# Edge masks as PE's stationary operand, sums turned back on PE, tree sums on DVE, and scatters after the degree loop, in a graph convolution kernel

## The chip, the cores and the metric

The kernel runs on one core of one Trainium2 chip. The metric is the device time of one execution in microseconds (us). The core has five engines with queues of their own: PE (TensorE, matmuls and weight loads), DVE (VectorE), ACT (ScalarE), POOL (GpSimd) and SP (SyncE, which here only issues DMAs). They wait for each other through semaphores: an instruction waits until a counter has a value, and a finished instruction adds to one. A difference of 0.5% (15.5 us) is about what a measurement of this kernel can tell from none.

## The reference

```python
def gcn_conv(x, src, dst, w, W, b, n):
    xw = x @ W
    deg = jax.ops.segment_sum(w, dst, num_segments=n)
    dinv = jnp.where(deg > 0, jax.lax.rsqrt(deg), 0.0)
    norm = dinv[src] * w * dinv[dst]
    return jax.ops.segment_sum(xw[src] * norm[:, None], dst, num_segments=n) + b
# gnn: edges + one loop edge of weight 1 for each node
out = relu(gcn_conv(x, src, dst, w, W1, b1, n))
out = gcn_conv(out, src, dst, w, W2, b2, n)
out = relu(batch_norm(out) * gamma + beta + identity)
# all: x is (6250, 256) float32; 100000 edges, dst sorted
x = x + gnn(layernorm(x), edges)
# ffn: softmax over 8 experts, the two best, gelu, hidden size 512
x = x + ffn(layernorm(x))
```

## The kernel before

The 6250 nodes are 49 tiles of 128 rows. The 100000 edges, sorted by target, are tiles of 128, and 14 edge tiles (`GT`) are a group; there are 56 groups, and each one's targets lie within 128 nodes. The product with `W` comes after the sum over edges, so a layer is: scale the nodes' rows (`y`), store them as a table in DRAM, sum over edges into `acc` in SBUF (features on partitions, nodes along the columns), and multiply.

The 56 groups are summed in two ways. 16 of them (`DG`) are *dense*: a matrix of pair weights (`pairs` in DRAM, first filled with zeros by SP, then POOL *scatters* each edge's weight into its cell, L479, 224 scatters of 128 cells) is loaded by SP in *units* (L374, `load_pairs`, 256 KB each, seven slots ahead), and PE multiplies the node rows by it (L1272, two matmuls of 128x512 a unit, 196 units a layer). As several edges may fall into one cell, DVE first sums the weights of edges with equal source and target (the *pair sums*, L781 to L791): for 40 distances, eight at a time in five chunks, it compares keys (L781), multiplies by the weights (L783) and reduces, by maximum to learn whether an edge's cell has been had before (L784) and by sum for the weights (L787).

The other 40 groups (`GG`) are *sparse*: POOL *gathers* the source rows (L492, 14 gathers of 128 rows a group, into one of two halves of `G`), DVE builds for each edge tile a 128x128 *mask* of weights by target (L908), and PE multiplies (L1287): the gathered rows are the weights that PE holds, two blocks of 128 columns, and the mask moves. The sum comes out with features on partitions, and DVE adds it into `acc` (L932). POOL's gathers of group k wait until the sum of group k-2 is done (`summed`), PE's start of group k until that sum is added (`added`). The first 28 gathers of a layer wait for no sum.

Order on PE within a layer: the *self-turn* (L1260, 98 transposes that turn `y` tiles for the loop edges; DVE copies each out, L901, and PE waits for the copy of the tile two back), then `BEFORE` dense units, then the groups, with `PER_GROUP` units spread between a group's edge tiles. Before all this come the pair sums, the splits of edge weights into bf16 parts (L829, L832), and the *degree loop*: 56 half-turns in which DVE prepares a group (L842, L843, L845) and PE multiplies (L1224, 14 small matmuls), two buffers, each half waiting for the other engine. Then the scales (L851 to L890), `y` (L895 on DVE, L611 on ACT), the table's store on SP (L381), and POOL's gathers after that store. POOL's scatters wait only for the cell numbers (`cells_set`, L807) and the zeros (`filled`). The order is written out by hand in each engine's program.

## Time and profile before

| what | value |
|---|---|
| median of 3 runs | 3099.36 us (3092.58 to 3104.66) |
| the profiled execution | 3096.93 us, its span 3095.1 us |
| PE, matmuls | 2158.0 us busy, 70% of the span |
| PE, weight loads | 1539.0 us, 50% (beside the matmuls) |
| POOL | 1676.4 us, 54% |
| DVE | 901.8 us, 29% |
| ACT | 377.0 us, 12% |
| mean granted clock of PE | 0.889 of full speed |

The span in the page's order of time: edges loaded, pair sums and splits to 122.8 us; degree loop to 470; `y` stored to 490; self-turn and first dense units to 673.7, when the first group's sum is added; the groups of layer 0 to 1450, of layer 1 to 2354 (its own self-turn and gathers start at 1508); batch norm, layer norm, router and the expert layers to the end. "Busy" counts an engine's execution of instructions, not its waits. In rows of time, the bracket names how long the engine was idle before the instruction and what released it; "remote" is a release whose source the profile doesn't know, "issue" means that it waited for nothing that the profile shows.

### The profile page before, as it was taken

To read this page: it belongs to the slowest core of one execution; us is meant where nothing else is said; L and a number is where in the kernel's file an instruction comes from. 1 tells how busy PE (TensorE), PEld (TensorE's weight loads), DVE (VectorE), ACT (ScalarE), POOL (GpSimd) and SP (SyncE) were. 2 spreads that over 40 slices of the span, in tenths; PEclk is the share of its full clock that TensorE was granted. 3 is DMA by queue.
4 is the path that set the end of the run, shared out by engine and by line. 5 is a ranking of instruction groups with operands and counts; after the bars stand their busy time and mean duration, and the time that the engine had idled before them with its cause. 6 is when DMAs were issued, how large, how long until landed. Compare 5 with 4: busy or idle time off the path is not lost.

```text
span 3095.1 us, 34624 instructions
## 1 busy us (share of the span) xinstructions
PE 2158.0 (70%) x10692; PEld 1539.0 (50%) x10693; DVE 901.8 (29%) x2587; ACT 377.0 (12%) x1053; POOL 1676.4 (54%) x1782
## 2 busy tenths in 40 slices
PE   0100046998888788646598788888888666899897
PEld 0100033455555555535365455555555562788887
DVE  8700055011222211212332212222123676233332
ACT  6000001000000000001200000000000562333333
POOL 1677703016666666663346666666665430566665
PEclk9999999998888888767889899999999755999999
DMA  9940005544544444332445555555555023677775
GB/s 325 329 144 1 0 0 163 158 136 143 145 145 141 143 142 144 95 92 80 131 123 158 147 154 157 156 155 155 153 160 168 24 77 103 169 189 175 180 176 135
DMA packets 264392, 431.24 MB, mean 139 GB/s; under 512 B 39664, under 2 KB 147887, under 8 KB 264143
## 3 DMA queue, kind: packets, MB, share of 16 engines
q1 hardware_dynamic: 181455, 253.80, 26.1%
q0 software_dynamic: 81088, 173.80, 21.9%
q10 hardware_dynamic: 1728, 2.13, 0.2%
q8 instruction: 64, 1.05, 0.1%
q14 instruction: 57, 0.47, 0.0%
HBM read 339.36 MB, written 91.16 MB: 139 GB/s over the span
## 4 chain that ended last, share of the span: by engine, by line
another core or an unknown queue 28%; PE 23%; POOL 17%; DVE 13%; issue 11%; DMA 6%; POOLq 1%; DVEq 1%; SPq 1%; ACT 1%; ACTq 0%
POOL arena L492 14%; PE psum L1272 8%; PE psum L1287 4%; DMA ACC<-rows_for_experts,ACC 4%; DVE arena L908 3%; PE psum L1308 3%; PE psum L1394 2%; PE psum L1402 2%; POOL out_dram L558 2%; PE psum L1369 2%; DMA out_dram<-ACC 1%; PE psum L1224 1%; DVE ACC L845 1%; PE psum L1322 1%
## 5 line engine op out<-in xcount | busy, mean ns | idle before, releaser
L492 POOL DMA_INDIRECT arena<-conv_rows,edge_cols x1120 | 1059.4, 946 | 887.7 <-issue 318.7
L1287 PEld LDWEIGHTS psum<-arena 128*128 128x128 f32 x4480 | 640.9, 209 | 501.6 <-issue 484.8
L1287 PE MATMUL psum<-arena 128*128 128x128 f32 x4480 | 683.4, 296 | 289.9 <-issue 277.3
L1272 PE MATMUL psum<-arena,X 128*128 128x512 f32 x1568 | 815.5, 653 | 43.6 <-DVE ACC L923 26.4
L1272 PEld LDWEIGHTS psum<-arena,X 128*128 128x128 f32 x1568 | 303.3, 211 | 307.3 <-issue 273.3
L932 DVE TENSOR_TENSOR ACC<-ACC,psum 128x256 f32 x80 | 33.8, 422 | 1226.0 <-remote 1085.4
L479 POOL DMA_INDIRECT pair_weights<-scale_b,mean_b x224 | 229.5, 1025 | 156.3 <-DVE mean_b L807 88.3
L908 DVE TENSOR_SCALAR arena<-iota,edge_cols 128x128 f32<-128x128 f32 x1120 | 294.4, 370 | 0.3
L1224 PE MATMUL psum<-ACC 128*128 128x6 bf16 x784 | 56.1, 202 | 318.1 <-DVE ACC L845 299.0
L1394 PE MATMUL psum<-ACC,arena 128*128 128x128 f32 x1680 | 215.8, 284 | 0.2 <-DVE ACC L1154 0.2
L1224 PEld LDWEIGHTS psum<-ACC 128*128 128x128 bf16 x784 | 51.5, 159 | 322.8 <-DVE ACC L845 303.2
L558 POOL DMA_INDIRECT out_dram<-ACC x105 | 167.7, 1597 | 74.2 <-issue 49.2
L1394 PEld LDWEIGHTS psum<-ACC,arena 128*128 128x128 f32 x1680 | 206.8, 201 | 0.6 <-issue 0.6
L1402 PE MATMUL psum<-arena,ACC 128*128 x840 | 199.9, 381 | 0.2 <-ACT ACC L689 0.2
L1402 PEld LDWEIGHTS psum<-arena,ACC 128*128 128x128 f32 x840 | 152.7, 192 | 17.2 <-issue 0.6
L546 POOL DMA_INDIRECT ACC<-rows_for_experts,ACC x105 | 104.9, 999 | 84.8 <-DVE ACC L1141 51.0
L623 ACT ACTIVATE X<-tmp,dinv 128x256 f32<-128x256 f32 x49 | 24.9, 508 | 991.1 <-DVE tmp L971 991.1
L689 ACT ACTIVATE ACC<-psum,b1e 128x128 f32<-128x128 f32 x420 | 119.8, 369 | 164.5 <-PE psum L1394 130.8
L632 ACT ACTIVATE edge_cols<-ACC 128x256 f32 x49 | 18.8, 413 | 915.4 <-DVE ACC L992 914.8
L1172 DVE TENSOR_TENSOR ACC<-psum,b2e 128x256 f32<-128x256 f32 x105 | 44.7, 426 | 267.9 <-PE psum L1402 211.8
L842 DVE COPY ACC<-psum 128x6 f32 x56 | 9.1, 162 | 275.0 <-remote 263.2
L1260 PE MATMUL psum<-ident,X 128*128 128x128 f32 x196 | 50.3, 384 | 52.0 <-DVE ACC L901 27.3
(259 smaller groups left out, 1410.3 us busy)
## 6 DMA issues: line engine op xcount, KB each, us to landing
arena<-pair_weights SPq DMA_DIRECT2D x392, 256.0 KB
arena<-in_L_ffn_W_dram SPq DMA_DIRECT2D x113, 512.0 KB, 7.8
pair_weights<-zeros SPq DMA_DIRECT2D x4, 12544.0 KB, 60.5
arena<-conv_rows,edge_cols POOLq DMA_INDIRECT x1120
conv_rows<-X SPq DMA_DIRECT2D x14, 896.0 KB, 4.8
X<-in_x_dram SPq DMA_DIRECT2D x12, 896.0 KB, 10.4
rows_for_experts<-ACC SPq DMA_DIRECT2D x7, 910.0 KB, 4.3
out_dram<-X SPq DMA_DIRECT2D x6, 896.0 KB
```

The costliest lines, as they stand in the source:

```text
L479: pool.indirect_dma_start(pairs, bass.IndirectOffsetOnAxis(cell_i[:, t:t + 1], 0), cell_w[:, t:t + 1], None).then_inc(paired[b], 16)
L492: pool.indirect_dma_start(G[:, n * D:(n + 1) * D], None, y_tab[layer], bass.IndirectOffsetOnAxis(srcT[:, t:t + 1], 0)).then_inc(gathered[n ...
L546: pool.indirect_dma_start(xs[:, u * DX:(u + 1) * DX], None, rows_x, bass.IndirectOffsetOnAxis(slot_i[:, n:n + 1], 0)).then_inc(xs_in[u], 16)
L558: pool.indirect_dma_start(out, bass.IndirectOffsetOnAxis(slot_i[:, n:n + 1], 0), ys[:, u * D:(u + 1) * D], None, bounds_check=N - 1, oob_i ...
L689: ins = a.activation(hT[:, slot * H + c * P:slot * H + (c + 1) * P], psum[:, 2 + slot, c * P:(c + 1) * P], ACT.Gelu, bias=b1e[:, bass.ds(e ...
L908: v.tensor_scalar(S[:, n * P:(n + 1) * P], iota[:, 0:P], dst_rel[:, t:t + 1], wT[:, t:t + 1], ALU.is_equal, ALU.mult).then_inc(s_ready, 1)
L1224: ins = m.matmul(bank(2 + h, 6), hot[:, :, j], w_group[:, (h * GT + j) * 6:(h * GT + j + 1) * 6], start=(j == 0), stop=(j == GT - 1))
L1272: ins = m.matmul(bank(6 + c, BW), X[:, t * D + c * P:t * D + (c + 1) * P], A_in[:, u * BW:(u + 1) * BW], start=(t == 0), stop=(t == NT - 1))
L1287: ins = m.matmul(bank(2 * (k % 2) + c, P), G[:, n * D + c * P:n * D + (c + 1) * P], S[:, n * P:(n + 1) * P], start=(j == 0), stop=(j == GT ...
L1308: ins = m.matmul(bank(6 + j % 2, D), acc[:, k, bass.ds(q * P, P)], W[:, k * D:(k + 1) * D], start=(k == 0), stop=(k == KC - 1))
L1394: ins = m.matmul(psum[:, 2 + s, c * P:(c + 1) * P], w1s[:, s4 * KC * H + k * H + c * P:s4 * KC * H + k * H + (c + 1) * P], xsT[:, s * D + ...
L1402: ins = m.matmul(bank(4 + s, D), hT[:, s * H + c * P:s * H + (c + 1) * P], w2e[:, bass.ds(e * (HC * D) + c * D, D)], start=(c == 0), stop= ...
```

## The change

Four things, none of which alters what is computed.

1. *Tree sums.* In each of the five chunks the two reductions (L784, L787) become trees of element-wise instructions that halve the eight rows three times: maxima in bf16, sums in f32, and each chunk is joined to a running result, so that L789 to L791 fall away and one copy (L815 after) follows.
2. *The scatters wait for the degrees.* POOL's first scatter also waits for `deg_summed`, which DVE sets behind the degree loop.
3. *Masks as weights.* In a sparse group the mask is PE's stationary operand and the gathered rows move: one 128x256 matmul for each edge tile (L1320 after) instead of two of 128x128. The sum then has nodes on partitions. ACT copies it out of PSUM (L628, new), PE turns it with two transposes (L1306, new, behind the fifth edge tile of the next group), and DVE adds the turned sum (L955). DVE's masks of group k+1 wait for the sum of group k-1.
4. *Dense units.* `BEFORE` goes from 74 to 98 units in layer 0, `PER_GROUP` from 4 to 3.

```diff
-        BEFORE = (74, 0)
-        PER_GROUP = (4, 5)
+        BEFORE = (98, 0)
+        PER_GROUP = (3, 5)
...
                     pool.wait_ge(cells_set, 1)
+                    pool.wait_ge(deg_summed, 1)
...
+                def copy_sums(layer):
+                    for k in range(GG):
+                        act.wait_ge(summed, GG * layer + k + 1)
+                        if GG * layer + k >= 2:
+                            act.wait_ge(sum_turned, GG * layer + k - 1)
+                        a.activation(tmp[:, k % 2 * D:(k % 2 + 1) * D], bank(k % 2, D), ACT.Copy).then_inc(sum_copied, 1)
...
                 for c in range(MAXIN // 8):
...
-                    chain(v.tensor_reduce(had[0:DR, c * RW:(c + 1) * RW],
-                                          sliding(eq8[0:DR, :], HALO - d0, 8, SPAN - 1, RW).rearrange("p d i -> p i d"),
-                                          AX_X, ALU.max))
-                    chain(v.tensor_reduce(parts[0:DR, c * RW:(c + 1) * RW], wsame.rearrange("p d i -> p i d"),
-                                          AX_X, ALU.add))
...
+                    chain(v.tensor_tensor(had3[:, 0:4], sliding(eq8[0:DR, :], HALO - d0, 4, SPAN - 1, RW),
+                                          sliding(eq8[0:DR, :], HALO - d0 + 4 * (SPAN - 1), 4, SPAN - 1, RW), ALU.max))
+                    v.tensor_tensor(had3[:, 4:6], had3[:, 0:2], had3[:, 2:4], ALU.max)
+                    chain(v.tensor_tensor(wsame[:, 0:4], wsame[:, 0:4], wsame[:, 4:8], ALU.add))
...
+                v.tensor_copy(had_f[0:DR, :], had[0:DR, :]).then_inc(pairs_summed, 1)
...
                         def add_group(k):
-                            dve.wait_ge(summed, GG * layer + k + 1)
+                            dve.wait_ge(sum_turned, GG * layer + k + 1)
...
-                            v.tensor_tensor(a, a, psum[:, 2 * (k % 2):2 * (k % 2) + 2, 0:P], ALU.add).then_inc(added, 1)
+                            v.tensor_tensor(a, a, bank(2 + k % 2, D).rearrange("p (c n) -> p c n", c=KC), ALU.add).then_inc(added, 1)
...
                             if k + 1 < GG:
+                                if k:
+                                    dve.wait_ge(summed, GG * layer + k)
                                 build(k + 1)
...
+                        def turn_sum(k):
+                            pe.wait_ge(sum_copied, GG * layer + k + 1)
+                            if GG * layer + k >= 2:
+                                pe.wait_ge(added, GG * layer + k - 1)
+                            for c in range(KC):
+                                ins = m.transpose(bank(2 + k % 2, D)[:, c * P:(c + 1) * P],
+                                                  tmp[:, k % 2 * D + c * P:k % 2 * D + (c + 1) * P], ident[:, :])
+                            ins.then_inc(sum_turned, 1)
...
                             if GG * layer + k >= 2:
-                                pe.wait_ge(added, GG * layer + k - 1)
+                                pe.wait_ge(sum_copied, GG * layer + k - 1)
...
-                                for c in range(KC):
-                                    ins = m.matmul(bank(2 * (k % 2) + c, P), G[:, n * D + c * P:n * D + (c + 1) * P],
-                                                   S[:, n * P:(n + 1) * P], start=(j == 0), stop=(j == GT - 1))
+                                ins = m.matmul(bank(k % 2, D), S[:, n * P:(n + 1) * P], G[:, n * D:(n + 1) * D],
+                                               start=(j == 0), stop=(j == GT - 1))
                                 if j == GT - 1:
                                     ins.then_inc(summed, 1)
+                                if k and j == 4:
+                                    turn_sum(k - 1)
...
+                        turn_sum(GG - 1)
```

PE, layer 0, from the self-turn (L1260, after it L1285) to the first groups; L1272 (L1297) is a dense unit's matmul, L1287 (L1320) an edge tile's, and so many of a kind as stand behind x. Before:

```order
L1260 MATMUL psum<-ident,X 128x128 x98
L1263 COMPARE_AND_BRANCH
L1272 MATMUL psum<-arena,X 128x512 x148
L1287 MATMUL psum<-arena 128x128 x8
L1272 MATMUL psum<-arena,X 128x512 x2
L1287 MATMUL psum<-arena 128x128 x6
L1272 MATMUL psum<-arena,X 128x512 x2
L1287 MATMUL psum<-arena 128x128 x8
```

And after, to the second group's turn of the first group's sum:

```order
L1285 MATMUL psum<-ident,X 128x128 x98
L1288 COMPARE_AND_BRANCH
L1297 MATMUL psum<-arena,X 128x512 x196
L1320 MATMUL psum<-arena 128x256 x5
L1297 MATMUL psum<-arena,X 128x512 x2
L1320 MATMUL psum<-arena 128x256 x5
L1297 MATMUL psum<-arena,X 128x512 x2
L1320 MATMUL psum<-arena 128x256 x4
L1297 MATMUL psum<-arena,X 128x512 x2
L1320 MATMUL psum<-arena 128x256 x5
L1306 MATMUL psum<-ident,tmp 128x128 x2
```

48 dense matmuls have moved ahead of the first group, each group has half as many matmuls for its edge tiles, and the turn stands inside the next group, with the rest of that group queued behind it.

POOL, from the first scatter (`pair_weights`) to the gathers of the third group (`arena<-conv_rows`), with what each waits for. Before:

```order
L479 DMA pair_weights<-scale_b,mean_b 12873728x1 [waits filled0,cells_set]
L479 DMA pair_weights<-scale_b,mean_b 12873728x1 x55
```

After:

```order
L484 DMA pair_weights<-scale_b,mean_b 12873728x1 [waits filled0,deg_summed,cells_set]
L484 DMA pair_weights<-scale_b,mean_b 12873728x1 x55
L484 DMA pair_weights<-scale_b,mean_b 12873728x1 [waits filled1]
L484 DMA pair_weights<-scale_b,mean_b 12873728x1 x55
L484 DMA pair_weights<-scale_b,mean_b 12873728x1 [waits filled2]
L484 DMA pair_weights<-scale_b,mean_b 12873728x1 x55
L484 DMA pair_weights<-scale_b,mean_b 12873728x1 [waits filled3]
L484 DMA pair_weights<-scale_b,mean_b 12873728x1 x55
```

Only the first wait has changed; behind it stand all 224 scatters and then, in the same queue, every gather.

DVE, two successive groups: the masks (`arena<-iota,edge_cols`) of the next group, then the addition of this one's sum. Before:

```order
L908 TENSOR_SCALAR arena<-iota,edge_cols 128x128 x14
L912 TENSOR_LOAD base_i
L912 ISA x2
L932 ISA [waits dense_added,added,summed]
L932 TENSOR_TENSOR ACC<-ACC,psum 128x2x128
```

After:

```order
L931 TENSOR_SCALAR arena<-iota,edge_cols 128x128 [waits summed]
L931 TENSOR_SCALAR arena<-iota,edge_cols 128x128 x13
L935 TENSOR_LOAD base_i
L935 ISA x2
L955 ISA [waits dense_added,added,sum_turned]
```

The addition waits for PE's turn instead of PE's sum, and the masks have a wait of their own.

## Rows read from the trace of the kernel before

**Rows 1.** The page's chain of work that ended last: its first line.
```profile
another core or an unknown queue 28%; PE 23%; POOL 17%; DVE 13%; issue 11%; DMA 6%; POOLq 1%; DVEq 1%; SPq 1%; ACT 1%; ACTq 0%
```

**Rows 2.** Order of time, DVE, degree loop. Columns: start, duration (us), ..., [idle before, releaser].
```profile
299.07 0.16 DVE L842 COPY ACC<-psum 128x6 f32 x1 [37.81 <-remote]
...
338.28 0.17 DVE L842 COPY ACC<-psum 128x6 f32 x1 [37.86 <-remote]
...
429.95 0.16 DVE L842 COPY ACC<-psum 128x6 f32 x1
...
431.24 0.16 DVE L842 COPY ACC<-psum 128x6 f32 x1
...
431.50 1.09 DVE L845 TENSOR_TENSOR ACC<-ACC 128x1792 bf16<-128x1792 bf16 x1
```

**Rows 3.** Order of time, POOL: first and last of 224 scatters, first gather.
```profile
97.26 1.28 POOL L479 DMA_INDIRECT pair_weights<-scale_b,mean_b  x1 [88.27 <-DVE mean_b L807]
...
393.85 0.96 POOL L479 DMA_INDIRECT pair_weights<-scale_b,mean_b  x1 [0.30 <-issue]
...
499.43 0.99 POOL L492 DMA_INDIRECT arena<-conv_rows,edge_cols  x1 [104.63 <-DMA conv_rows<-X]
```

**Rows 4.** Order of time, DVE: two of the self-turn's 49 copies.
```profile
509.97 0.42 DVE L901 COPY ACC<-psum 128x256 f32<-128x256 f32 x1 [0.41 <-PE psum L1260]
...
523.88 0.42 DVE L901 COPY ACC<-psum 128x256 f32<-128x256 f32 x1 [2.37 <-remote]
```

**Rows 5.** Order of time, PE: 42 dense units (168 matmul records).
```profile
540.46 74.92 PE L1272 MATMUL psum<-arena,X 128*128 128x512 f32 x168 [4.65 <-DMA arena<-pair_weights]
```

**Rows 6.** Order of time, POOL: first gather after each of four waits for a sum.
```profile
673.74 0.94 POOL L492 DMA_INDIRECT arena<-conv_rows,edge_cols  x1 [139.00 <-PE psum L1287]
...
693.93 0.94 POOL L492 DMA_INDIRECT arena<-conv_rows,edge_cols  x1 [3.00 <-remote]
...
1299.76 0.94 POOL L492 DMA_INDIRECT arena<-conv_rows,edge_cols  x1 [2.73 <-remote]
...
1341.97 0.94 POOL L492 DMA_INDIRECT arena<-conv_rows,edge_cols  x1 [7.48 <-PE psum L1287]
```

**Rows 7.** Order of time, PE: the last matmuls of one group.
```profile
806.13 1.50 PE L1287 MATMUL psum<-arena 128*128 128x128 f32 x12
```

**Rows 8.** Order of time, DVE: two additions of a group's sum.
```profile
815.17 0.42 DVE L932 TENSOR_TENSOR ACC<-ACC,psum 128x256 f32 x1 [16.27 <-remote]
...
1311.94 0.42 DVE L932 TENSOR_TENSOR ACC<-ACC,psum 128x256 f32 x1 [8.31 <-remote]
```

**Rows 9.** Busy time (and count) of each engine in two stretches, core 0.
```profile
795.03:807.63 12.60, 12.60 (x66) 9.50 (x66) 3.87 (x15) 0.00 (x0) 9.50 (x11) 0.87 0.61 178
1299.76:1306.00 6.24, 5.97 (x38) 5.78 (x36) 3.88 (x15) 0.00 (x0) 4.72 (x5) 0.71 0.29 84
```

**Rows 10.** Order of time, DVE: pair sums, splits, first degree copy.
```profile
64.93 2.69 DVE L781 TENSOR_TENSOR ACC<-arena 112x2432 f32<-112x2432 f32 x1
...
67.66 2.29 DVE L783 TENSOR_TENSOR arena<-ACC,arena 112x2048 f32<-112x2048 f32 x1
...
69.87 3.61 DVE L784 TENSOR_REDUCE ACC<-ACC 112x256 f32<-112x2048 f32 x1
...
89.36 2.31 DVE L789 TENSOR_REDUCE ACC<-ACC 112x256 f32<-112x1280 f32 x1
...
93.93 0.43 DVE L791 TENSOR_TENSOR arena<-arena 112x256 f32<-112x256 f32 x1
...
104.78 7.97 DVE L829 TENSOR_TENSOR ACC<-ACC 128x784 bf16<-128x784 bf16 x3
...
122.76 0.17 DVE L842 COPY ACC<-psum 128x6 f32 x1 [2.01 <-issue]
```

**Rows 11.** The page's groups: busy us, mean ns | idle before, releaser.
```profile
L1287 PE MATMUL psum<-arena 128*128 128x128 f32 x4480 | 683.4, 296 | 289.9 <-issue 277.3
...
L623 ACT ACTIVATE X<-tmp,dinv 128x256 f32<-128x256 f32 x49 | 24.9, 508 | 991.1 <-DVE tmp L971 991.1
```

More of the change, by code:

```diff
@@ L109, in gnn_ffn @@
         eqw = arena[:, at:at + 8 * RW]
-        parts = arena[:, at + 8 * RW:at + (8 + MAXIN // 8) * RW]
-        assert (8 + MAXIN // 8) * RW <= 2 * GT * P
+        wsum = arena[:, at + 8 * RW:at + 9 * RW]
+        cell, hop = [arena[:, at + (9 + n) * RW:at + (9 + n) * RW + DT] for n in range(2)]
+        assert 11 * RW <= 2 * GT * P
         at += 2 * GT * P
@@ L143, in gnn_ffn @@
         tile_f = early(2 * NG)
-        eq8 = early(8 * (HALO + RW))
-        had = early(MAXIN // 8 * RW)
+        eq8 = early(8 * (HALO + RW), BF16)
+        had8 = early(8 * RW, BF16)
+        had, had_f = early(RW, BF16), early(RW)
+        int_f = early(2 * RH)
         assert at <= KC * NP
@@ L612, in _ @@
                                      bias=nb[:, t:t + 1], scale=sc[:, t:t + 1]).then_inc(y0_act, 1)
+                act.wait_ge(flag_set, 1)
+                general = act.value_load(flag_i[0:1, 0:1], min_val=0, max_val=1)
+                def copy_sums(layer):
[4 more added lines that the diff above has]
+                        a.activation(tmp[:, k % 2 * D:(k % 2 + 1) * D], bank(k % 2, D), ACT.Copy).then_inc(sum_copied, 1)
+                with act.If(general == 0):
+                    copy_sums(0)
+                act.wait_ge(agg_done, 1)
                 act.sem_inc(y_ready, 1)
@@ L624, in _ @@
                                      scale=dinv[:, t:t + 1]).then_inc(y_ready, 1)
+                with act.If(general == 0):
+                    copy_sums(1)
                 with act.Fori(0, NCH) as c:
@@ L750, in _ @@
                 dve.wait_ge(ld_rows, 16 * ROW_LOADS)
-                seen, first = eq8[0:DR, 0:RH], eq8[0:DR, RH:2 * RH]
+                seen, first = int_f[0:DR, 0:RH], int_f[0:DR, RH:2 * RH]
                 v.tensor_copy(seen, src_h[0:DR, :])
@@ L1207, in _ @@
                 pe.wait_ge(pairs_summed, 1)
-                for x, rows in enumerate((eq8[0:DR, 0:RW], eqw[0:DR, RW:2 * RW])):
+                for x, rows in enumerate((had_f[0:DR, :], wsum[0:DR, :])):
                     for h in range(2):
```

12 lines of the change are left out of this document (8 added, 4 removed).

## The prediction, as put on record before the kernel was run

> **What bounds the kernel now.** I read the page's chain of waits first: 28% of the span ends on "another core or an unknown queue" on one core, 23% on PE, 17% on POOL, 13% on DVE [rows 1]. A release that the profile can't name, for over a quarter of the span, is the thing to explain. Then I read DVE, PE and POOL in order of time, stage by stage.
>
> *Degree loop.* Each of 56 half-turns is three DVE instructions (L842, L843, L845) and 14 small PE matmuls. Undisturbed, copies L842 follow each other by 1.29 us (429.95, 431.24); while POOL issues the scatters of L479, by 39.2 us (299.07, 338.28), 37.8 of them idle, "remote" [rows 2]. PE's work hasn't grown: what arrives late is its semaphore update. 39.2 us for 14 matmuls and 14 weight loads is 1.40 us per PE instruction. The scatters go out from 97.26 to 393.85, 224 of them, so one per 1.33 us (0.96 busy and 0.30 between in the clean part) [rows 3]. The loop only runs off when they end.
>
> *Self-turn.* It begins fresh on PE, and when POOL gathers from 499.43 on, a tile (two transposes, four PE records) goes, after some 12 us and 15 tiles, from 0.83 us (0.42 busy, 0.41 idle at 509.97) to 2.79 us (0.42 and 2.37 at 523.88) [rows 3, 4]: 0.70 us per PE record. So the lateness again, at half the rate.
>
> *Dense units, then the first sum.* 42 units take 74.92 us, 1.78 each [rows 5]. POOL's third gather group waits 139 us for the first sum, to 673.74 [rows 6].
>
> *Groups.* POOL restarts every 20.2 us (673.74, 693.93): 14 gathers of 1.25 = 17.2 to the end of the last, then 3.00 "remote" [rows 6]. The sum that it waits for is long done: in a like group its last matmul ends at 806.13+1.50 = 807.63, but DVE adds at 815.17 [rows 7, 8]. From POOL's restart at 795.03 to that last matmul PE ran 66 matmul and 66 weight-load records [rows 9]. Where the dense units are over, a sum comes earlier in POOL's stream, within its first 74 records [rows 9], and DVE adds at 1311.94 [rows 8]: late too, but before the 14 gathers are out; POOL then runs two groups on end, 1299.76 to 1341.97, with a pause of 7.48 [rows 6]. So the picture is: in a stream of POOL's issues the first some 70 PE records are answered within 12 to 16 us, later ones 0.7 to 1.4 us apiece, and what is left when POOL stops. The period is set by POOL's issues plus that flush, and PE's own work matters through its number of records, not its length.
>
> The Trainium skill (SBUF — State Buffer, "Who interferes with whom") says that PE and ACT never wait on anyone. Here DVE waits 37.8 us for a PE that has 14 short matmuls to do. If the rule held also for these updates, the first rival below is what comes.
>
> **The change part by part.** All sums are made against the profiled execution, 3096.93 us, 0.1% under the median of 3099.36.
>
> *Tree sums (DVE, on the path to the scatters and the degree loop).* A chunk is L781 2.69, L783 2.29, L784 and L787 some 3.6 each: 12.2 us, five times, then L789 and its twin L790 at 2.3 and L791 0.43 [rows 10]. After: L802 and L804 stay; four f32 adds of 1024, 512, 256 and 256 columns, at L783's 1.12 ns a column and some 0.13 each to start (256 columns took 0.43), are 2.8 us; four bf16 maxima of the same sizes are 1.7 us at L845's rate (1792 columns in 1.09) or 2.8 at f32's [rows 2, 10]. A chunk is 9.5 to 10.6; times five saves 8 to 14; at the end 5.0 become 0.4, 4.6 more. 13 to 19; I take 16, between the two. The Trainium skill (VectorE: DVE Perf Modes, "Mode 2×_1P — pack two bf16 into one 32-bit read") asks for 4-byte alignment, and the first maximum's operands begin at odd columns: by it the maxima would be nearer the dear end, which L845's aligned row can't show.
> The splits after it (L829, L832, six of 2.66 [rows 10]) lay beside scatters; L845's rate gives 0.5 for 784 columns. 0 to 13 less; I take 5. The degree loop starts at 122.76−21 = 102 [rows 10].
>
> *Scatters wait for the degrees.* Degree loop 102 + 56×1.29 + 1.4 ≈ 176. Scatters then, 224×1.263 = 283 us: to 459. The 28 gathers that wait for no sum are behind them in POOL's queue, and y is stored by then: to 494, flushed 3 us later. Queued behind POOL's wait is every gather; the pair loads on SP wait for the scatters block by block (56 each, the first at 247).
> PE meanwhile: before, the self-turn began 14.5 us after the loop's end, so at 190, now under the scatters. Some 15 tiles pass promptly (10 us), 34 tiles of four records go at 1.40 or 0.70: 190 or 95 us, to 390 or 295. A dense unit has eight records, 11.2 or 5.6 us: by 494 9 or 35 units, and some 7 more are in flight. 82 or 56 of the 98 are left, ×1.78 = 146 or 100, and 9 for the rest of the first group: first sum at 652 or 606, against 673.6. The row for a stream of scatters is the 1.40 one; I take 640, **−33**. What covers the 283 us of scatters before is the degree loop, which is held; after, only self-turn and dense, held likewise: a shift of work under the same cover.
>
> *Masks as weights, sums copied and turned.* Per group before: 4480/80 = 56 matmul records and as many weight loads [rows 11], 112, and 32 for dense; now 56 in all, 24 dense, 4 to turn. ACT's copy is about 0.51 (L623, 128x256 f32 [rows 11]), the turn and DVE's add under a microsecond each. Nothing is queued behind ACT's wait but later copies. PE's turn, though, stands after the fifth tile of the next group, and everything of that group is behind it; DVE's masks wait for the sum before. Since PE, blocked at a turn until POOL stops, starts fresh, the next sum is about 60 records into POOL's stream, where it is answered before the 14 gathers are out: POOL runs two groups (28×1.25 = 34.7) and pauses 3.0 (as at 693.93) to 7.5 (as at 1341.97): 18.85 to 21.1 a group. In the latter PE had slow passes to make up, so I take a pause of 4.1, 19.4: 0.8×32 groups = **−26**, three more for the last groups. In layer 1 there are five dense units, 64 records to the sum, and the mask build is held by the turn; two-group and one-group streams mix (38.5+20.2)/3 = 19.6; between 18.85 and 20.5; I take 19.95 for 40 groups, **−10**. At each layer's end copy, turn and add come behind the last sum, 1.5 each: **+3**.
> The longer matmul (256 columns for two of 128) moves as many columns, and POOL's issues, not PE, make the period: nothing. If it cost PE half as much again, that is below 3 us a group (28 matmul records of 0.1 us more each, a third of their mean 0.296 [rows 11]), inside POOL's 17.
>
> Sum: 3096.9−33−26−3−10+3 = **3028 us**.
>
> **Rivals.**
> *A, PE isn't held under scatters that it doesn't read* (held only where a handshake has to come back, say). For: nothing but the half-rate under gathers. Against: 39.2. Self-turn and dense end by about 404, the first sum at 495 when its gathers have landed: −178, with the periods' −36 and +3, 2885.
> *B, slower: the price is per handshake, not per record.* Each half-turn of the degree loop is one PE update that DVE needs, 39 us. The self-turn has one per tile. Then from 190 to 494 only eight tiles pass beyond the prompt 15; after 497 there are 26×0.83 = 22, 98×1.78 = 174 and 9: first sum at 702, +28, no gain in the periods (each group has two more such updates), +3: 3128. For it: nobody but the degree loop measured the scatters. Against: the self-turn's 2.8 us under gathers, one per tile too. It decides when more than about 167 us of PE's work is left at 497.
> *C, the groups stay at 20.2* (PE's turn makes POOL's next sum late as before; each stream 14 gathers): 3096.9−33+3 = 3067. For it: in every stretch with dense units POOL paused after each group.
> *D, the added links lengthen the groups* to the 21.1 of the two-group stream with its 7.48 pause: 3067 + 0.8×72 = 3124.
> *E, POOL never pauses*, 17.5 a group: −2.7×72 = −194, with −33 and +3, 2873.
>
> **How the numbers follow.** Forecast 50%, C 30%, B 8%, A 5%, D 4%, E 3%. Its own range: −67 to −22 for the first sum, −43 to −10 and −54 to +0 for the periods, 2936 to 3068. The range given, 2945 to 3100, takes in C and its upper end; left out are A and E below, B and D above. 0.5% of 3099 (15.5 us) is what a measurement can tell from no change: faster is the forecast, C less its worst, A and E, 80%; same 8%, slower 12%, B and D.
>
> **What would show it.** DVE's degree copies all 1.29 apart; POOL's first scatter at about 176, its first gather right behind the last scatter (459). DVE's self-turn copies 2.8 or 5.6 us apart from about 200 on. First wait for a sum ending at 606 to 652. POOL's gathers in streams of 28 with pauses of 3 to 5 in layer 0. Wrong: copies 39 us apart in the self-turn (B), one pause per 14 gathers (C), a dense part that is over by 404 (A).

## The result, and the profile after

The changed kernel takes 3116.87 us (median of 8 runs, 3112.64 to 3129.26), the one before 3101.02 us (8 runs): ratio 1.0054, 95% interval 1.0034 to 1.0075. It is slower by half a per cent; the forecast was 3028, with a range of 2945 to 3100. The profiled executions' spans are 3115.6 and 3095.1 us, 20.5 apart.

| point in the span (us) | before | after | difference |
|---|---|---|---|
| first scatter | 97.26 | 177.65 | +80.4 |
| degree loop over | 470 | 176 | −294 |
| first gather | 499.43 | 464.93 | −34.5 |
| POOL restarts on the first sum | 673.74 | 690.63 | +16.9 |
| last sum of layer 0 added | 1449.76 | 1453.86 | +4.1 |
| first gather of layer 1 | 1507.76 | 1514.73 | +7.0 |
| last sum of layer 1 added | 2356.67 | 2377.26 | +20.6 |
| end | 3095.1 | 3115.6 | +20.5 |

So 34.5 us gained at the first gather are lost again before the first sum, and 16.9 more; layer 0 gives 12.8 back, layer 1 costs 13.6, the linear stage between them 2.9. The page's chain of waits after (compare [rows 1]):

```profile
PE 31%; another core or an unknown queue 19%; POOL 18%; issue 14%; DVE 9%; DMA 6%; ACT 1%; POOLq 1%; DVEq 1%; SPq 1%; ACTq 0%
```

PE has taken over first place from the nameless releaser, 31% against 23% before, and the nameless share is down from 28% to 19%. The granted clock is no part of the difference: the eight executions have a mean of 0.79 (3112.6 to 3117.4 us) or 0.85 (3114.7 to 3129.3), and 17 executions of the kernel before on one chip, at 0.81 (3088.6 to 3100.7) or 0.89 (3083.2 to 3103.3), don't differ by it either. POOL in order of time (start, duration, engine, line, [idle before, releaser]), the answers to [rows 3, 6]:

```profile
177.65 1.17 POOL L484 DMA_INDIRECT pair_weights<-scale_b,mean_b  x1 [168.64 <-DVE ACC L876]
...
463.67 0.96 POOL L484 DMA_INDIRECT pair_weights<-scale_b,mean_b  x1 [0.30 <-issue]
...
464.93 1.00 POOL L497 DMA_INDIRECT arena<-conv_rows,edge_cols  x1 [0.30 <-issue]
...
690.63 0.95 POOL L497 DMA_INDIRECT arena<-conv_rows,edge_cols  x1 [187.22 <-PE psum L1320]
...
730.59 0.95 POOL L497 DMA_INDIRECT arena<-conv_rows,edge_cols  x1 [5.05 <-remote]
...
750.65 0.95 POOL L497 DMA_INDIRECT arena<-conv_rows,edge_cols  x1 [2.80 <-remote]
...
1973.28 0.95 POOL L497 DMA_INDIRECT arena<-conv_rows,edge_cols  x1 [17.16 <-PE psum L1320]
```

The scatters start at 177.65 (176 was forecast), the gathers follow at once, and the restart is at 690.63, not 640. A stream of 28 gathers is followed by a pause of 5.05, one of 14 by 2.80. POOL is slowed as well at the end of this long stream: its last 25 DMAs are 1.40 us apart and 1.10 busy, where it had been 1.27 and 0.96.

```profile
502.33 1.09 POOL L497 DMA_INDIRECT arena<-conv_rows,edge_cols  x1 [0.30 <-issue]
```

DVE, from the pair sums through the splits and the degree loop to the self-turn [rows 2, 4, 10]:

```profile
64.34 2.69 DVE L802 TENSOR_TENSOR ACC<-arena 112x2432 bf16<-112x2432 f32 x1
...
67.07 2.29 DVE L804 TENSOR_TENSOR arena<-ACC,arena 112x2048 f32<-112x2048 bf16 x1
...
69.28 0.69 DVE L805 TENSOR_TENSOR ACC<-ACC 112x1024 bf16<-112x1024 bf16 x1
...
71.60 0.29 DVE L809 TENSOR_TENSOR ACC<-ACC 112x256 bf16<-112x256 bf16 x1
...
84.27 7.96 DVE L852 TENSOR_TENSOR ACC<-ACC 128x784 bf16<-128x784 bf16 x3
...
102.24 0.17 DVE L865 COPY ACC<-psum 128x6 f32 x1 [2.00 <-issue]
...
103.54 0.16 DVE L865 COPY ACC<-psum 128x6 f32 x1
...
194.52 0.42 DVE L924 COPY ACC<-psum 128x256 f32<-128x256 f32 x1 [0.41 <-issue]
...
225.53 0.42 DVE L924 COPY ACC<-psum 128x256 f32<-128x256 f32 x1 [5.16 <-remote]
...
404.73 0.42 DVE L924 COPY ACC<-psum 128x256 f32<-128x256 f32 x1 [5.17 <-remote]
...
410.34 0.42 DVE L924 COPY ACC<-psum 128x256 f32<-128x256 f32 x1 [5.18 <-issue]
...
421.53 0.42 DVE L924 COPY ACC<-psum 128x256 f32<-128x256 f32 x1 [5.17 <-remote]
```

The degree loop (L865) runs at 1.30 us a half-turn. The self-turn's copies (L924) come every 5.6 us, 404.73 to 410.34: four PE records of 1.40. PE's dense units in the same stretch [rows 5]:

```profile
491.47 3.78 PE L1297 MATMUL psum<-arena,X 128*128 128x512 f32 x4 [7.42 <-DMA arena<-pair_weights]
...
502.51 3.42 PE L1297 MATMUL psum<-arena,X 128*128 128x512 f32 x4 [7.25 <-DMA arena<-pair_weights]
...
531.16 59.38 PE L1297 MATMUL psum<-arena,X 128*128 128x512 f32 x132 [3.86 <-DMA arena<-pair_weights]
...
593.62 86.08 PE L1297 MATMUL psum<-arena,X 128*128 128x512 f32 x196 [3.08 <-DVE ACC L946]
```

A dense unit (x4) comes every 11.0 us (491.47 to 502.51): eight records of some 1.40, though the idle time is put down to the unit's load. That goes on until 531, 27 us after the end of POOL's last gather of this stream (502.33 + 1.09 = 503.4). Then 33 units and, after the block's addition, 49 more are left, 82.

Last, POOL's steady stretch by windows (busy time and count of PE, PE's weight loads, DVE, ACT and POOL, then the granted clock, the DMA share and GB/s): 37 groups (518 gathers) in each layer, in layer 1 after the change 36 (505). After:

```profile
690.63:1429.84 739.21, 502.14 (x1504) 310.68 (x1502) 152.36 (x563) 14.21 (x38) 492.47 (x518) 0.79 0.42 124
1577.29:2321.32 744.03, 599.83 (x1818) 352.21 (x1816) 150.51 (x552) 13.84 (x37) 479.45 (x505) 0.87 0.51 153
```

Before:

```profile
673.74:1424.89 751.15, 563.15 (x2579) 395.61 (x2578) 153.78 (x568) 0.00 (x0) 490.28 (x518) 0.82 0.45 130
1570.52:2324.70 754.18, 629.22 (x2829) 411.24 (x2828) 153.67 (x568) 0.00 (x0) 489.68 (x518) 0.92 0.53 155
```

That is 19.98 us a group instead of 20.30 in layer 0, and 20.6 instead of 20.4 in layer 1, with the granted clock down from 0.82 and 0.92 to 0.79 and 0.87. PE's matmul records fell from 2579 to 1504, and the period moved by 0.3 us.

### The profile page after: what moved, and what is told of

It is laid out like the page before. It is cut to its first block, busy times and chain, and to the rows that moved or that the text cites. A ratio compares the mean times of both kernels' runs of the same rounds, so it can differ in the third digit from the quotient of the medians.

```text
span 3115.6 us, 30733 instructions
## 1 busy us (share of the span) xinstructions
PE 2147.3 (69%) x8612; PEld 1417.5 (45%) x8613; DVE 881.2 (28%) x2615; ACT 408.5 (13%) x1133; POOL 1674.2 (54%) x1782
## 4 chain that ended last, share of the span: by engine, by line
PE 31%; another core or an unknown queue 19%; POOL 18%; issue 14%; DVE 9%; DMA 6%; ACT 1%; POOLq 1%; DVEq 1%; SPq 1%; ACTq 0%
POOL arena L497 16%; PE psum L1297 13%; PE psum L1320 6%; DMA ACC<-rows_for_experts,ACC 4%; PE psum L1344 3%; PE psum L1430 2%; PE psum L1438 2%; PE psum L1405 2%; POOL out_dram L563 1%; DVE arena L931 1%; DMA out_dram<-ACC 1%; DVE ACC L868 1%; PE psum L1249 1%; PE psum L1358 1%
## 5 line engine op out<-in xcount | busy, mean ns | idle before, releaser
L1297 PE MATMUL psum<-arena,X 128*128 128x512 f32 x1568 | 819.2, 650 | 195.7 <-issue 95.3
L1320 PE MATMUL psum<-arena 128*128 128x256 f32 x2240 | 631.2, 413 | 203.0 <-issue 174.8
L1320 PEld LDWEIGHTS psum<-arena 128*128 128x128 f32 x2240 | 457.4, 208 | 445.7 <-issue 368.1
L1297 PEld LDWEIGHTS psum<-arena,X 128*128 128x128 f32 x1568 | 319.6, 207 | 517.3 <-issue 383.6
L955 DVE TENSOR_TENSOR ACC<-ACC,psum 128x256 f32 x80 | 33.8, 422 | 1247.9 <-remote 802.9
L484 POOL DMA_INDIRECT pair_weights<-scale_b,mean_b x224 | 217.9, 973 | 237.7 <-DVE ACC L876 168.6
L628 ACT ACTIVATE tmp<-psum 128x256 f32<-128x256 f32 x80 | 30.7, 384 | 2093.4 <-remote 1089.6
L1285 PE MATMUL psum<-ident,X 128*128 128x128 f32 x196 | 53.2, 380 | 231.7 <-issue 136.8
L1285 PEld LDWEIGHTS psum<-ident,X 128*128 128x128 f32 x196 | 25.6, 182 | 258.8 <-issue 252.1
L924 DVE COPY ACC<-psum 128x256 f32<-128x256 f32 x98 | 40.2, 423 | 243.0 <-remote 196.1
L1306 PE MATMUL psum<-ident,tmp 128*128 128x128 f32 x160 | 36.0, 311 | 77.6 <-ACT tmp L628 70.1
L946 DVE TENSOR_TENSOR ACC<-ACC,psum 128x256 f32 x32 | 13.5, 420 | 265.4 <-PE psum L1297 256.3
```

The costliest lines, as they stand in the source:

```text
L484: pool.indirect_dma_start(pairs, bass.IndirectOffsetOnAxis(cell_i[:, t:t + 1], 0), cell_w[:, t:t + 1], None).then_inc(paired[b], 16)
L1285: ins = m.transpose(bank(4 + t % 2, D)[:, k * P:(k + 1) * P], X[:, t * D + k * P:t * D + (k + 1) * P], ident[:, :])
L1297: ins = m.matmul(bank(6 + c, BW), X[:, t * D + c * P:t * D + (c + 1) * P], A_in[:, u * BW:(u + 1) * BW], start=(t == 0), stop=(t == NT - 1))
L1320: ins = m.matmul(bank(k % 2, D), S[:, n * P:(n + 1) * P], G[:, n * D:(n + 1) * D], start=(j == 0), stop=(j == GT - 1))
```

## The experiments

The theory drawn from this trace (theory 1) is that what POOL issues is finished more slowly than POOL issues it, one DMA per 1.40 (scatters) to 1.43 us (gathers) against 1.26 and 1.25, and that while the surplus is open, PE's updates come one by one behind it. It would explain at once why the hold outlasts a stream by a time that grows with the stream's length: 2.80 after 14 gathers, 5.05 after 28, 27 after 252 DMAs. It also gives 14 × 1.43 = 20.0 for a group with either form of matmul. The rivals: PE is held for as long as POOL issues at all (theory 3, the prediction's); the wait alone cost the 17 us (theory 2). Runs of one letter share a chip, on which the kernel before ran as well, so ratios are compared, not times.

### Taking the wait away, or putting only it in; issuing more slowly

The run e1 takes the wait out of the changed kernel, and e4 puts it alone into the kernel before:

```diff
                     pool.wait_ge(cells_set, 1)
-                    pool.wait_ge(deg_summed, 1)
```

e2 and e3 put a small instruction behind every DMA of POOL; `paced` counts only POOL's own memsets:

```diff
+                def breathe(times):
+                    for _ in range(times):
+                        pool.wait_ge(paced, count[0])
+                        g.memset(pace[:, :], 0.0).then_inc(paced, 1)
+                        count[0] += 1
...
                         pool.indirect_dma_start(pairs, bass.IndirectOffsetOnAxis(cell_i[:, t:t + 1], 0),
                                                 cell_w[:, t:t + 1], None).then_inc(paired[b], 16)
+                        breathe(1)
```

> The changed kernel without the scatters' wait for the degree loop; all else as changed. Theory 1 (POOL's DMAs are finished one per 1.40 to 1.45 us whatever else runs, 252 of them from 177.65 to 531 in the changed kernel; POOL issues one per 1.26, and while that surplus is open PE's semaphore updates come one at a time behind it): scatters from about 76, their surplus gone at about 400, degree loop off at about 450, first sum 21 us earlier than in the kernel before for the tree sums and 41 later for the 24 dense units ahead of it: 693, so about as changed (690.6): 3114 to 3122. Theory 2 (the wait is what cost the 17 us up to the first sum): 674 or less, 3098.

Measured 1.0092 (1.0063 to 1.0121), 3127 us, a little above theory 1's 3122; first restart 699.1. The wait is not what cost: without it the kernel is no faster (the two intervals touch), where theory 2 had 3098. Theory 2 falls.

> The kernel before with only the scatters' wait for the degree loop. Theory 1: scatters from about 197 on, 252 DMAs of 1.40 to 550; held self-turn (5.6 us a tile) and some 10 dense units under it; 57 of the 74 units left, 100 us: first sum at about 665 instead of 673.7, 3085 to 3095. Theory 2: it costs 17 us, 3116.

Measured 0.9964 (0.9941 to 0.9987), first restart 668.5 against 665 by theory 1. Alone, the wait gains 11 us.

> The changed kernel with a small memset (128x96, with a wait on the one before it, which is long done) on POOL behind every scatter and every gather, so that POOL issues one DMA per about 1.5 us instead of 1.26. Theory 1: no surplus builds up and PE is never held; self-turn and dense units run at PE's own rate under the scatters, first sum at about 540 instead of 690.6, and POOL gathers without pauses, 21 us a group instead of 20.0: end of layer 0 near 1358 (1454 now), layer 1 about 20 shorter: 3000 (2980 to 3040). Theory 3 (PE is held record by record for as long as POOL issues at all, as my prediction had it): the holding only gets longer, +60 and more for the first sum and 3 us a group: 3200 or more.

Measured 0.9844 (0.9811 to 0.9876), 3051, first restart 641.45. The memset fitted in large part into the 0.30 us between two issues, so the spacing rose only to 1.31 us between gathers and 1.33 between most scatters; with some slower ones the scatters' mean is 1.40. DVE's self-turn copies show a hold that comes and goes, 4.47 and 1.00 us of idle time within ten microseconds:

```profile
223.90 0.42 DVE L936 COPY ACC<-psum 128x256 f32<-128x256 f32 x1 [3.09 <-remote]
...
237.22 0.42 DVE L936 COPY ACC<-psum 128x256 f32<-128x256 f32 x1 [4.47 <-remote]
...
246.39 0.42 DVE L936 COPY ACC<-psum 128x256 f32<-128x256 f32 x1 [1.00 <-PE psum L1297]
```

And POOL's restarts, each after 28 gathers:

```profile
641.45 0.95 POOL L508 DMA_INDIRECT arena<-conv_rows,edge_cols  x1 [111.47 <-PE psum L1332]
...
681.46 0.95 POOL L508 DMA_INDIRECT arena<-conv_rows,edge_cols  x1 [3.36 <-remote]
...
721.39 0.95 POOL L508 DMA_INDIRECT arena<-conv_rows,edge_cols  x1 [2.99 <-remote]
```

40.0 us for 28 gathers at 1.31, as it is 40.0 at 1.25 (690.63 to 730.59): POOL's pace changed, the time of a group did not. The expectation was missed (3000, at most 3040): the 21 us a group and the 540 rested on a spacing of 1.5, which this wasn't. The direction is theory 1's, and theory 3 (3200) is out.

> Both: no wait of the scatters for the degree loop, and the memset behind every scatter and gather. Theory 1: scatters from 76 to 412, the degree loop beside them at 1.3 us a half-turn, first sum at about 440, POOL without pauses at 21 us a group: end of layer 0 near 1256, in all about 2900 (2870 to 2950). Theory 3: the degree loop is held till the scatters end, later than now: 3200 or more.

Measured 0.9723 (0.9677 to 0.9770), the least certain of the numbers: the four executions spread from 3004 to 3076 us, the ratio rests on the two shortest, and the profiled one took 3050. Expected was 2900, and missed. At 1.33 the degree loop was still held under the scatters, late in it up to 28 us a half-turn, so that it ended at 414 instead of some 175; POOL's first gather came at 443.6 and its restart at 655.0.

### Above 1.40

Two memsets (of 32 columns) make most scatters 1.44 us apart (1.45 in the mean in f1; 1.54 and 1.55 in f2 and f3, where the first ones run beside the degree loop). One memset of 32 columns, as f2 has it behind its gathers, disappears in the 0.30: the gathers stay at 1.26.

> The changed kernel (with the scatters' wait) with two small memsets behind each scatter, about 1.55 us apart instead of 1.26 (one memset made it 1.31, still under 1.40); gathers not paced. Theory 1 (1.40 us a DMA, PE held only while POOL is ahead): self-turn copies at most 0.9 us apart under the scatters, none at 5.6; the 98 dense units done before the scatters end; scatters to about 524, gathers to 560, first sum at about 545 instead of 690.6; later stages as changed: about 2970 (2950 to 2990). Theory 3 (PE is held record by record while POOL issues, less when it issues more slowly): one memset took the first sum to 641, a second as much again to 620 at best: 3045 or more.

Measured 0.9634 (0.9611 to 0.9657). DVE's self-turn copies under the scatters, and PE's dense units and first group:

```profile
205.29 0.85 DVE L935 COPY ACC<-psum 128x256 f32<-128x256 f32 x2 [0.42 <-issue]
...
214.16 0.86 DVE L935 COPY ACC<-psum 128x256 f32<-128x256 f32 x2 [0.41 <-issue]
```

```profile
263.50 87.34 PE L1308 MATMUL psum<-arena,X 128*128 128x512 f32 x196 [39.11 <-DMA arena<-pair_weights]
...
353.92 86.08 PE L1308 MATMUL psum<-arena,X 128*128 128x512 f32 x196 [3.08 <-DVE ACC L957]
...
509.40 2.04 PE L1331 MATMUL psum<-arena 128*128 128x256 f32 x4 [69.40 <-DMA arena<-conv_rows,edge_cols]
```

Two copies every 1.27 us, where it had been 5.6 for one; 98 units done by 440, and PE now waits 69 us for POOL's first gather. With the scatters 0.18 us further apart each, 224 times, their stretch is some 40 us longer, and the kernel 4.2% (130 us) shorter, ratio against ratio. The first sum was expected at 545 and the kernel at 2970 (0.958): POOL stops only after 42 gathers here and restarts at 564.5, since the gathers, unpaced, hold PE as before.

The same stretch tests the wording of theory 1. PE takes the gathers in pairs as they land: it starts on the first pair at 509.40 (above) and on the tenth at 531.90.

```profile
531.90 0.81 PE L1331 MATMUL psum<-arena 128*128 128x256 f32 x2 [1.39 <-DMA arena<-conv_rows,edge_cols]
```

The second gather of these pairs was issued at

```profile
506.51 0.96 POOL L508 DMA_INDIRECT arena<-conv_rows,edge_cols  x1 [0.88 <-issue]
...
529.05 0.95 POOL L508 DMA_INDIRECT arena<-conv_rows,edge_cols  x1 [0.30 <-issue]
```

That is 2.89 us from issue to PE for the second gather and 2.85 for the twentieth. Finished one per 1.43 us, the twentieth would have been 3 us later than that. So the gathers themselves land as fast as POOL issues them; what lags by 0.18 us for each DMA is something else, which no run here shows. From here on theory 1 is only the rule of counting that it gave: 1.40 to 1.43 us for each DMA until PE is free.

> The kernel before with two memsets behind each scatter, nothing else. Theory 1: scatters from 97 to 444, degree loop beside them, over by about 200; first sum at about 470 instead of 673.7; groups as before: about 2895 (2880 to 2930). Theory 3: 3090 or more.

Measured 0.9351 (0.9330 to 0.9372), 2924.7. First restart 484.0 instead of 673.7 (470 and 2880 to 2930 were expected). The degree loop is nearly free: most half-turns are 1.3 us, some 2.3 to 3.8, and it ends at 213.6. This is the largest effect of the study, in the kernel before, with two memsets a scatter and nothing else.

> The changed kernel without the scatters' wait for the degree loop, two memsets behind each scatter, one behind each gather. Theory 1: scatters from 75 to about 422, degree loop beside them at 1.3 us a half-turn, y stored near 200, gathers straight behind the scatters, first sum at about 447; 20.0 us a group; about 2870 (2850 to 2920). Theory 3: the degree loop is held by the scatters as with one memset, first sum at about 640, 3030.

Measured 0.9358 (0.9333 to 0.9382), 2919.9; first restart 461.9 (447 was expected). All of the change but its wait brings nothing over the kernel before once the scatters are paced.

### The masks part, and the tree sums

f4 is the changed kernel with the masks part undone (on DVE, ACT and PE, back to the lines of before):

```diff
-                                ins = m.matmul(bank(k % 2, D), S[:, n * P:(n + 1) * P], G[:, n * D:(n + 1) * D],
-                                               start=(j == 0), stop=(j == GT - 1))
+                                for c in range(KC):
+                                    ins = m.matmul(bank(2 * (k % 2) + c, P), G[:, n * D + c * P:n * D + (c + 1) * P],
+                                                   S[:, n * P:(n + 1) * P], start=(j == 0), stop=(j == GT - 1))
...
-                                if k and j == 4:
-                                    turn_sum(k - 1)
```

> The changed kernel with the masks part undone (gathered rows as weights, no copies on ACT, no turns, DVE adds the sum itself); tree sums, the scatters' wait and 98 units ahead stay. Theory 1 (a group is 14 DMAs of 1.43 us with either form): first sum at about 692, 20.2 us a group in both layers, layer 1 as before (907 us from the end of layer 0, instead of 923): 3108 to 3116, so the masks part by itself is worth nothing or costs a few us. Theory 4 (the masks part makes layer 0's groups 12.8 us shorter in all and that is its whole effect): 3127.

Measured 1.0036 (1.0016 to 1.0055), first restart 689.5, as theory 1 had it (692, and 3108 to 3116 are 1.003 to 1.0055), against 1.0054 for the changed kernel: the intervals overlap. A pair on one chip settles it: tree sums alone (i2), and tree sums with the masks part (i1, the changed kernel without the wait and with 74 and 4 units).

> The kernel before with only the tree sums, again. With the hold 0.993 to 0.995; without it 0.992 as measured.

Measured 0.9948 (0.9922 to 0.9973).

> The changed kernel without the scatters' wait and with 74 and 4 dense units as before (so tree sums and masks part only). With the hold: 24 units fewer ahead of the first group (43 us) than in the run of the changed kernel without the wait (ratio 1.009): 0.995 to 1.0. Without it: POOL's unbroken run 21 us earlier and nothing else in the way, 0.992, as with tree sums only.

Measured 0.9994 (0.9974 to 1.0013). Side by side: first restart at 660.5 with the masks part and 660.9 without it; layer 0's last sum added at 1438.3 and 1439.4; layer 1, from there to its own last sum, 933.4 and 905.4 us. The masks part gives one microsecond in layer 0 and costs 28 in layer 1 (these two profiled executions are 30 us apart, the medians 16.6, so 28 is a high reading of it). What costs in layer 1 can be seen in the changed kernel, DVE first, then PE:

```profile
1960.86 0.42 DVE L955 TENSOR_TENSOR ACC<-ACC,psum 128x256 f32 x1 [33.12 <-remote]
...
1967.04 0.42 DVE L946 TENSOR_TENSOR ACC<-ACC,psum 128x256 f32 x1 [0.39 <-DVE ACC L946]
```

```profile
1967.51 2.93 PE L1297 MATMUL psum<-arena,X 128*128 128x512 f32 x3 [11.83 <-DVE ACC L946]
```

In a stream of 28 gathers DVE has waited 33 us when the first group's turned sum reaches it. The addition of a dense block (L946) stands behind it in DVE's order, PE's next dense unit waits for that addition 11.8 us, and POOL, waiting for PE, pauses 17.16 (its row at 1973.28 above). Layer 1 has three such places behind gathers; in layer 0 two of the four blocks are added before the first group. But the kernel before has such waits too. PE's three in layer 1 are 11.02, 6.11 and 1.75 us there and 9.10, 11.83 and 3.35 here; in i1 two come to 22.2 us, in i2 there is one of 9.1. The rows of POOL show two further parts. Its ten other pauses after 28 gathers (without the layer's first, 27.8), some 5.1 us each in layer 0, are 5.1 to 8.3 in layer 1, 62.3 in all, 11 to 12 us more than ten of 5.1. And from layer 1's last gather to its last sum added it is 22.1 us here and 15.7 before (in i1 22.5, in i2 16.1). Of the 13.6 us that layer 1 costs in the changed kernel, 6.4 stand there, and the other 7.2 between its first gather and its last (840.4 us, 833.2 before).

### Chips without the hold

The next two sets met chips on which the kernel before takes 2612.87 and 2608.72 us.

> The changed kernel with the masks part undone and the scatters' wait taken out, two memsets behind each scatter (that is the kernel before with the tree sums and 98 units ahead, scatters paced). Theory 1: as the kernel before with paced scatters (first sum seen at 484, ratio 0.935), 20 us less for the tree sums: ratio 0.929. Against the next run it shows what the masks part is worth when nothing is held under the scatters: if it costs (layer 1 was 923.1 us with it and 906.9 without it on one chip), this run is the faster one by 3 to 10 us.

> The changed kernel without the scatters' wait, two memsets behind each scatter, gathers not paced. Theory 1: ratio 0.932 to 0.936; 20 us a group in streams of 28 and 14 gathers; layer 1 some 14 us longer than in the run with the old masks. Theory 4 (the masks part shortens layer 0 by some 13 us and costs layer 1 nothing of its own): faster than the run with the old masks.

> As the last, with two memsets behind each gather as well, so gathers 1.44 us apart. Theory 1 (1.43 us a gather is what is finished anyway, issued at 1.25, 1.31 or 1.44): no pauses, 14 x 1.44 = 20.2 us a group, PE and DVE see every sum at once; no long pauses at the dense blocks in layer 1, tails shorter: layer 1 ten to fifteen shorter, ratio 0.925 to 0.935. If the pauses are a price for each wait instead of a backlog, they stay at 3 us on top of 20.2: ratio 0.99.

> The kernel before with two memsets behind each scatter and each gather. Theory 1: no pauses, 20.2 us a group: like the kernel before with only the scatters paced (ratio 0.935), at most ten less, 0.932 to 0.937. A price for each wait: 0.99.

Measured 1.0130 (1.0113 to 1.0146), 1.0144 (1.0121 to 1.0167), 1.0957 (1.0937 to 1.0977) and 1.0986 (1.0968 to 1.1005): all four expectations missed, since they were for the other kind of chip. So gathers 1.44 us apart, theory 1's best test of the groups, were never run on a chip with the hold. POOL goes from the first scatter to the last gather of layer 0 without one pause, so every memset is added. From the first scatter to the last gather of layer 0 it is 1050.4 us with paced scatters (g1) and 1000.0 with tree sums alone (h4 below); pacing 1120 gathers by 0.19 each is 213 us, and g3 is 215 over g2. The scatters' 224 × 0.18 are 40 of the 50 between g1 and h4.

> The changed kernel as it is. On a chip with the hold (kernel before near 3100): +0.5%. On one without it (near 2613): POOL there issues scatters and gathers without a pause from its first scatter to the last gather of layer 0, so the 80 us by which the scatters' wait delays the first one (97 to 177) come straight on top: 2693 or a little over, ratio 1.025 to 1.035.

Measured 1.0289 (1.0268 to 1.0311), 2684.1. The chain's first line, and DVE's self-turn under unpaced scatters with the first group's sum:

```profile
POOL 50%; issue 18%; PE 13%; DVE 9%; DMA 7%; POOLq 1%; ACT 1%; DVEq 0%; SPq 0%; ACTq 0%
```

```profile
219.91 0.85 DVE L924 COPY ACC<-psum 128x256 f32<-128x256 f32 x2 [0.41 <-PE psum L1285]
...
221.18 0.42 DVE L924 COPY ACC<-psum 128x256 f32<-128x256 f32 x1 [0.42 <-PE psum L1285]
...
489.48 0.42 DVE L955 TENSOR_TENSOR ACC<-ACC,psum 128x256 f32 x1 [54.47 <-PE psum L1306]
```

No hold at 1.26 us a scatter: two copies in 1.27 us, and the first group's sum is added at 489.48, where the changed kernel's first profile has 694.59. POOL is half of the chain, and the 80 us by which its first scatter is late come through almost whole (75).

> The kernel before with only the tree sums. The scatters start 21 us earlier (76 instead of 97). With the hold the degree loop, bound by the scatters, ends as much earlier: ratio 0.993 to 0.995. Without it POOL's unbroken run starts 21 us earlier: 0.992.

Measured 0.9917 (0.9892 to 0.9943). Its degree loop beside the scatters, DVE and POOL:

```profile
152.21 0.16 DVE L849 COPY ACC<-psum 128x6 f32 x1
...
153.52 0.17 DVE L849 COPY ACC<-psum 128x6 f32 x1
```

```profile
157.29 1.02 POOL L483 DMA_INDIRECT pair_weights<-scale_b,mean_b  x1 [0.30 <-issue]
...
158.62 0.96 POOL L483 DMA_INDIRECT pair_weights<-scale_b,mean_b  x1 [0.30 <-issue]
```

1.31 us a half-turn while POOL issues every 1.3; on the chip of the first profile a half-turn was 39.2 [rows 2]. This run also says where the difference between the chips lies. Its span is 2587.2 us, and the tree sums' 21 us added to that are 487 less than the 3095.1 of the kernel before. Of these, 345 stand between POOL's first scatter and its last gather of layer 0 (999.1 us against 1343.9), and 131 between the first and the last gather of layer 1 (702.4 against 833.2).

> The changed kernel with the masks part undone and no wait of the scatters, two memsets behind each scatter. With the hold: first sum seen near 470, 0.93 of before. Without it, 1.013 as measured: 224 x 0.18 = 40 us of memsets less some 20 for the tree sums.

> The changed kernel without the scatters' wait, two memsets behind each scatter. With the hold: 0.932 to 0.937, and some 5 us slower than the run before it if the masks part costs more in layer 1 (14) than it gives in layer 0 (8 to 13). Without it, 1.014 as measured.

Measured 1.0139 (1.0110 to 1.0169) and 1.0139 (1.0114 to 1.0165), as the second halves of the expectations have it: on such chips the masks part is worth nothing either.

Which version beats both? Tree sums alone do, on either kind of chip: 0.9948 and 0.9917. Paced scatters (0.935) are the better version only where the hold is. Where it isn't, g1, which has them with the tree sums and 98 units ahead, is at 1.0130 and the tree sums alone are at 0.9917, some 2% less; pacing alone was not run there.

## Why the prediction was wrong

The profiled execution was to be 69 us shorter and is 20.5 longer, 89.5 off: 49.9 at the first sum, 14.7 in the rest of layer 0, 2.9 between the layers, 22.1 in layer 1. Two steps failed: the end of the hold (34 us of the 49.9) and the groups' periods (36.8 us in both layers).

*The tree sums: right, and under-sized.* A chunk is 9.3 us (64.34 to the next stage at 73.65), cells come 20.8 us earlier (97.26 to 76.5 in e1) instead of 16, the degree loop starts at 102.24 (102 forecast). The four maxima are 0.69, 0.43, 0.29 and 0.29, the 1.7 of the cheap end. The first one has operands at odd columns and still runs 1024 columns in 0.69 us, near L845's rate (1.09 for 1792). The alignment that the Trainium skill (VectorE: DVE Perf Modes, "Mode 2×_1P — pack two bf16 into one 32-bit read") asks for, and by which I leaned away from that end, did not show here. The splits did not get cheaper without scatters beside them (L852, 2.65 each, as before): that 5 was a misreading, and by luck made up for the other.

*The scatters' wait: the mechanism right, "flushed 3 us later" wrong.* This is the first step that failed. 5.6 us a tile and 11.2 a unit are as forecast (1.40 per record, so the price is per record and B falls; A, by which nothing would be held, falls as well). But I took the end of the hold, 3 us after POOL's last issue, from streams of 14 gathers (the 3.00 at 693.93 [rows 6]). The trace of before had the answer for a long stream, and I had not put the two rows together: the last scatter is issued at 393.85 [rows 3], and DVE's degree copies read

```profile
415.28 0.17 DVE L842 COPY ACC<-psum 128x6 f32 x1 [36.46 <-remote]
...
420.98 0.16 DVE L842 COPY ACC<-psum 128x6 f32 x1 [4.32 <-remote]
...
422.25 0.16 DVE L842 COPY ACC<-psum 128x6 f32 x1
```

still held at 415.28, free from 421 on, 27 us later. So it was here: hold until 531, not 497, 34 us, with 82 units to go. 12 more are my choice of 640 where the slow end, the one that the scatters' own row spoke for, was 652; the other 5 are those units' clock and waits. The prompt start, too, was 7 tiles and not 15 (then the copies wait 1.9, 3.8, 4.5 us), so the self-turn ended at 421.5 instead of 390.

*98 units ahead of the first group: priced, but not seen as a loss.* On a chip with the hold the group takes 20 us with three dense units in it or four. 24 units of 1.78 us ahead cost 43 us before the first sum by this count, and little comes back behind it. The runs with 98 and with 74 units that are otherwise the same, e1 and i1, on different chips, agree in the main: the first restart is 38.6 us later (699.1 and 660.5), the last sum of layer 0 29 (1467.4 and 1438.3), and the ratio is up from 0.9994 to 1.0092, 30 us. Put one behind the other, the ratios give tree sums −16 us (i2), masks part +14 (i1), 24 units ahead +30 (e1), the wait −12 (the changed kernel): +17, the whole. Only the first two stand on one chip; the masks part is +6 by the changed kernel against f4, and the wait alone −11 (e4). Without the 24 units there would be no loss.

*The periods: "PE's records set the pause" wrong.* The forecast let the number of PE records decide: 60 to the next sum, so 28 gathers go out, so fewer pauses. The first two parts came true (streams of 28 are seen), the third not: the pause after 28 is 5.05, so that the group stays at 20.0. In layer 0 a pause is a time per DMA issued, about 0.18 us × their number, not a time per wait. This was rival C in size (20.2 kept) and it had 30%; the likeliest case had 4.1 where its own bounds were 3.0 and 7.5. In layer 1 the step "19.95" came out at 20.6: it missed the block addition before 1973.28 (17.16 instead of 5.1) and the longer pauses after 28 gathers, 6.2 us in the mean. Of the "1.5" at a layer's end, layer 1 has 6.4. Why the pauses are longer there, beside five dense units a group, stays open.

*The direction.* Rivals B and D held the slower side with 12%, and neither happened: no self-turn copy came 39 us after the last (B), and the groups did not go to 21.1 us (D). The 16 us came from a mechanism right in kind with an end 34 us late, from periods that hardly moved, and from units moved to where they cost.

## What to carry to other kernels

When an engine's idle time is "remote", measure how it grows: put the length of the stream that seems to cause it beside the time by which it outlasts that stream, for a short and for a long one, before pricing anything on the short one. If a steady period doesn't move when the work in it does, divide it by the number of the one thing that did not change (here 14 gathers, 1.43 us each). A unit of work moved out of a stretch that is bound elsewhere costs its full time where it goes and returns little. And measure on more than one chip before tuning against such an effect: two memsets a scatter gave 0.935 alone on one chip, and versions that had them were at 1.013 to 1.014 on two others.

## What the runs showed of the hardware

On three of the five chips that the experiments met, PE's semaphore updates come late while POOL issues indirect DMAs back to back. At a spacing of 1.26 us it is 1.40 us per PE record (5.6 us a self-turn tile of four). At 1.33 it comes and goes, 1.4 to 4.9 us a tile in e2. At 1.44 a tile takes 0.64 us in f1, and in f3 some half-turns of the degree loop still take 2.3 to 3.8 us instead of 1.3. The gathers themselves land in all this 2.85 to 2.89 us after their issue (f1). On the other two chips the effect is absent at 1.26, and the kernel before takes 2613 and 2609 us instead of 3100, 3125 and 3095. That is some 16% of its time; by h4 all but 11 us of the difference stand in the stretches in which POOL scatters and gathers. The Trainium skill (SBUF — State Buffer, "Who interferes with whom") has PE and ACT wait for nobody; the second kind of chip agrees (h1: a self-turn tile in 0.64 us under the scatters), and on the first PE's updates are late, of which that rule says nothing. What POOL's issues and PE's updates share, and why chips differ in it, no run shows.
